# Four score tiles at a time from row tiles, attention reordered by batch, router in column strips

## The reference

```python
q = layernorm(x) @ Wq.T;  k, v = split(ctx @ Wkv_expand.T)
scores = einsum('bhqd,bhkd->bhqk', q, k) / sqrt(32)      # causal, so 100 keys
x = x + tanh(g_xattn) * ((softmax(scores) @ v) @ Wout.T)
h = layernorm(x)
e = argmax(sigmoid(h @ router_w));  p = max(sigmoid(h @ router_w))
x = x + tanh(g_ffn) * p * ((silu(h @ gate_w[e]) * (h @ up_w[e])) @ down_w[e])
```

## Time and profile before

| | us |
|---|---|
| median of 3 runs | 558.25 (558.22 to 561.51) |
| the profiled run, its own time | 560.19 |
| its span, first to last instruction | 558.7 |
| TensorE busy | 508.5 (91%) |
| VectorE, ScalarE, GpSimd busy | 349.5, 303.6, 185.4 |

### The profile page before, as it was taken

How to read it: one execution, slowest core, us unless ns; L and a number is a source line. 1 busy time by engine, 2 the same in 40 slices (tenths; PEclk the granted TensorE clock), 3 DMA queues, 4 the chain that set the end, 5 groups by cost and what they waited for, 6 DMA issues and landing times.

```text
span 558.7 us, 11407 instructions
## 1 busy us (share of the span) xinstructions
PE 508.5 (91%) x3724; PEld 423.9 (76%) x3724; DVE 349.5 (63%) x745; ACT 303.6 (54%) x855; POOL 185.4 (33%) x210
## 2 busy tenths in 40 slices
PE   0999999999999999976489999999999999999991
PEld 0976686768665866656489999999999999999980
DVE  3678568756885556686446666757566665766731
ACT  0799648765786568522134554545454644545520
POOL 5534304631572147233532233224122241220211
PEclk9999999999999999995599999999999999999996
DMA  7500032103310031073428676887677797776610
GB/s 195 169 8 2 16 90 88 61 16 90 89 48 25 15 91 59 18 245 115 104 81 246 212 237 184 262 248 210 199 240 220 212 283 205 205 244 195 224 54 29
DMA packets 58910, 77.30 MB, mean 138 GB/s; under 512 B 5074, under 2 KB 40506, under 8 KB 58880
## 3 DMA queue, kind: packets, MB, share of 16 engines
q1 hardware_dynamic: 53728, 66.90, 40.2%
q0 software_dynamic: 5152, 10.03, 6.3%
HBM read 67.76 MB, written 10.34 MB: 140 GB/s over the span
## 4 chain that ended last, share of the span: by engine, by line
PE 71%; DVE 8%; issue 7%; ACT 6%; POOL 3%; DMA 3%; DVEq 0%; ACTq 0%; SPq 0%; POOLq 0%
PE bank L1148 20%; PE bank L1149 20%; PE bank L1150 19%; ACT pr L668 3%; POOL pn L508 3%; PE bank L1243 2%; PE bank L1233 2%; DMA staging<-in_L_xattn_Wq 2%; PE bank L1282 1%; PE bank L1402 1%; PE bank L1252 1%; ACT staging L612 1%; PE bank L1169 1%; PE bank L1290 1%; DVE pT L970 1%
## 5 line engine op out<-in xcount | busy, mean ns | idle before, releaser
L1148 PE MATMUL bank<-x_hi,gu_hi 128*128 128x224 f32 x512 | 142.6, 279 | 2.9 <-ACT qT L744 1.6
L1149 PE MATMUL bank<-x_lo,gu_hi 128*128 128x224 f32 x512 | 141.9, 277 | 0.0
L1150 PE MATMUL bank<-x_hi,gu_lo 128*128 128x224 f32 x512 | 140.3, 274 | 0.0
L1148 PEld LDWEIGHTS bank<-x_hi,gu_hi 128*128 128x128 f32 x512 | 99.2, 194 | 4.6 <-ACT qT L744 1.7
L1149 PEld LDWEIGHTS bank<-x_lo,gu_hi 128*128 128x128 f32 x512 | 99.2, 194 | 1.0
L1150 PEld LDWEIGHTS bank<-x_hi,gu_lo 128*128 128x128 f32 x512 | 99.3, 194 | 0.0
L668 ACT ACTIVATE pr<-bank,nmx 100x100 f32<-100x100 f32 x256 | 85.6, 374 | 15.5 <-DVE nmx L961 12.1
L781 DVE TENSOR_TENSOR gu_lo<-staging,gu_hi 128x1024 fp32r<-128x1024 f32 x64 | 76.6, 1221 | 16.7 <-ACT gu_hi L612 15.6
L612 ACT ACTIVATE gu_hi<-staging 128x1024 fp32r<-128x1024 f32 x64 | 65.7, 1050 | 31.9 <-DMA staging<-in_L_ffn_up_w 20.7
L508 POOL TENSOR_TENSOR pn<-pr,inv 100x400 f32<-100x400 f32 x64 | 54.6, 853 | 77.7 <-DVE inv L954 72.5
L668 ACT ACTIVATION_READ_ACCUMULATOR pr<-bank,nmx 100x1 f32 x256 | 60.2, 236 | 0.0
(11 more groups left out here) (182 smaller groups left out, 963.7 us busy)
## 6 DMA issues: line engine op xcount, KB each, us to landing
staging<-in_L_ffn_gate_w SPq DMA_DIRECT2D x32, 512.0 KB, 5.4
staging<-in_L_ffn_up_w SPq DMA_DIRECT2D x32, 512.0 KB, 7.2
staging<-in_L_ffn_down_w SPq DMA_DIRECT2D x32, 512.0 KB, 4.0
x_rows<-x SPq DMA_DIRECT2D x8, 800.0 KB
xt<-in_x SPq DMA_DIRECT2D x4, 800.0 KB
xr<-in_x SPq DMA_DIRECT2D x16, 200.0 KB
staging<-in_L_xattn_Wq SPq DMA_DIRECT2D x1, 1024.0 KB, 11.5
x<-in_L_xattn_Wout SPq DMA_DIRECT2D x1, 1024.0 KB, 9.7
```

Source lines behind the costliest of these rows:

```text
L1148: nc.tensor.matmul(dst, a[0], b[0], start=first, stop=False)
L1149: nc.tensor.matmul(dst, a[0], b[1], start=False, stop=False)
L1150: return nc.tensor.matmul(dst, a[1], b[0], start=False, stop=last)
```

## The change

Four things are done. **Scores:** keys are kept as they are (`kT`, one copy of 128 rows in place of four of 32 rows; both `memset`s go), and a head's scores are a product of depth 32 at its own row tile of the array. Tile `n` now holds head `r = n % 4` of each of the four 128-row groups; four banks take the four tiles of a batch, and `scores(c, i)` writes all four with 16 products, after four masks. The bank is gained by giving `out_b` one bank, and tokens always go through `misc_b`. **Order:** all lists of `attend` are rewritten batch by batch. **Router:** 16 products of 100 columns into four strips of 32 rows with a router widened by zeros, and one transpose of 128x128 in place of four small ones. **Stores:** the counter `rows_stored` becomes two, and `residual(c, 0)` waits for the second norm of the former chunk's rows.

```diff
@@ -94,8 +94,6 @@
     DEEP = 3
-    SOONER = 2
-    SPARE_FROM = 14
     KEEP = HP + 2
...
-        keys_b = staging[:, 0:KC * CB * HP * S].rearrange("p (m i j s) -> p m i j s", m=KC, i=CB, j=HP)
+        kT = staging[:, 2 * 3 * 1024 - KC * CT:].rearrange("p (m t) -> p m t", m=KC)
...
-        score_b, turn_b, out_b, misc_b = banks[0:3], banks[3:5], banks[5:7], banks[7]
+        score_b, turn_b, out_b, misc_b = banks[0:4], banks[4:6], banks[6], banks[7]
...
             def keep(c, t):
 
                 act.wait_ge(kq_ready.sem, kq_ready.after(c, t + 1))
-                m, bank = t // 2, score_b[(NT + t) % DEEP]
+                m, bank = t // 2, score_b[t % HP]
                 if t % 2 == 0:
-                    for j in range(HP):
-                        r = slice(j * HD, (j + 1) * HD)
-                        ins = copy(keys_b[r, m, :, j, :], bank[r, 0:CT].rearrange("p (i s) -> p i s", i=CB))
+                    ins = copy(kT[:, m, :], bank[:, 0:CT])
...
+                for n in range(NT):
+                    i, r = n // HP, n % HP
+                    exponentials(c, n)
+                    if n == 0:
+                        keep_values(c, CB - 1)
+                    if n in (1, 2, 4, 6) and not last:
+                        split_token(c + 1, n // 2 if n != 1 else 0)
+                    if n == 8 and not last:
                         split_context(c + 1)
...
+                    if 9 <= n < 9 + CB and not first:
+                        keep_normed(c - 1, n - 9)
+                    if r == 0 and i:
+                        split_output(c, i - 1)
+                    if n == 13 and not first:
                         exp_logits(c - 1)
...
-                dve.wait_ge(rows_stored.sem, rows_stored.after(c, 0))
-                nc.vector.scalar_tensor_tensor(out=x1[0:S, i, 0:H], in0=out_b[i % 2][0:S, :], scalar=tanh_x[0:S, 0:1],
+                dve.wait_ge(x1_stored.sem, x1_stored.after(c, 0))
+                if i == 0:
+                    dve.wait_ge(x2_done.sem, x2_done.after(c, 0))
+                nc.vector.scalar_tensor_tensor(out=x1[0:S, i, 0:H], in0=out_b[0:S, :], scalar=tanh_x[0:S, 0:1],
...
+                for i in range(CB):
+                    n = HP * i
+                    row_max(c, n)
+                    if i:
+                        keep_turned(c, n - 1)
+                    row_max(c, n + 1)
+                    if i == 1 and not first:
+                        rows_norm(c - 1, 12, NORM_STEPS)
+                    row_max(c, n + 2)
+                    inverse(c, n)
+                    row_max(c, n + 3)
+                    if i == 0 and not first:
+                        residual(c - 1, CB - 1)
+                    if i == 1 and not last:
+                        split_token(c + 1, 2)
+                    if i == 2 and not last:
                         split_context(c + 1)
...
+                    if i:
+                        low_output(c, i - 1)
+                    inverse(c, n + 1)
+                    keep_turned(c, n)
+                    if i == 0 and not first:
+                        rows_norm(c - 1, 0, 4)
+                    if i == 0 and not last:
+                        split_token(c + 1, 0)
+                    inverse(c, n + 2)
+                    keep_turned(c, n + 1)
+                    if i == 0 and not first:
+                        rows_norm(c - 1, 4, 8)
+                    if i < 2 and not last:
+                        split_token(c + 1, 1 + 2 * i)
+                    inverse(c, n + 3)
...
+                    keep_turned(c, n + 2)
+                    if i == 0 and not first:
+                        rows_norm(c - 1, 8, 12)
+                    if i and not (i == CB - 1 and last):
+                        residual(c, i - 1)
...
+                keep_turned(c, NT - 1)
+                if not first and not last:
+                    for k in range(CHOOSE_STEPS):
+                        settled(choose, c - 1, whole, k)
...
-            def scores(c, n):
-
-                i, m, b = n // KC, n % KC, n % DEEP
+            def mask_scores(c, n):
+
+                i, r = n // HP, n % HP
                 if n == 0:
                     pe.wait_ge(kq_done.sem, kq_done.after(c, 2 * KC))
-                if n >= DEEP:
-                    pe.wait_ge(exp_done.sem, exp_done.after(c, n - DEEP + 1))
-                nc.tensor.matmul(score_b[b][0:S, 0:HP * S], eye[0:S, 0:S], mask[0:S].unsqueeze(1).to_broadcast([S, HP, S]),
-                                 start=True, stop=False)
-                nc.tensor.matmul(score_b[b][0:S, 0:HP * S], qT[:, m, i * S:(i + 1) * S],
-                                 keys_b[:, m, i].rearrange("p j s -> p (j s)"), start=False, stop=True).then_inc(s_ready.sem, 1)
+                elif i:
+                    pe.wait_ge(exp_done.sem, exp_done.after(c, n - HP + 1))
+                nc.tensor.matmul(score_b[r][0:S, 0:KC * S], eye[0:S, 0:S], mask[0:S].unsqueeze(1).to_broadcast([S, KC, S]),
+                                 start=True, stop=False, skip_group_check=True)
+
+            def scores(c, i):
+
+                t = slice(i * S, (i + 1) * S)
+                for m in range(KC):
+                    for r in range(HP):
+                        p = slice(r * HD, (r + 1) * HD)
+                        ins = nc.tensor.matmul(score_b[r][0:S, m * S:(m + 1) * S], qT[p, m, t], kT[p, m, t], start=False,
+                                               stop=m == KC - 1, tile_position=(r * HD, 0), skip_group_check=True)
+                ins.then_inc(s_ready.sem, 1)
...
-                    ins = nc.tensor.matmul(whole.logits, router[:, k, :], x2T[:, k, :], start=k == 0, stop=k == KC - 1)
+                    for i in range(CB):
+                        ins = nc.tensor.matmul(whole.logits[i * HD:(i + 1) * HD, :], router_wide[:, k, :],
+                                               x2T[:, k, i * S:(i + 1) * S], start=k == 0, stop=k == KC - 1,
+                                               tile_position=(0, i * HD), skip_group_check=True)
...
+                for n in range(HP):
+                    mask_scores(c, n)
+                scores(c, 0)
+
+                if not first:
+                    project(c - 1, CB - 1)
+                values(c, CB - 1)
...
+                if not last:
+                    turn_chunk(c + 1, 0)
+                for i in range(CB):
+                    n = HP * i
+                    if i:
+                        turn_probs(c, n - 1)
+                    if i == 1 and not last:
+                        turn_chunk(c + 1, 2)
+                    if i == 2 and not last:
                         turn_context(c + 1)
...
+                    if i:
+                        weigh(c, i - 1)
...
+                    turn_probs(c, n)
+                    if i < CB - 1:
+                        mask_scores(c, n + 4)
+                    if i == 0 and not last:
+                        turn_chunk(c + 1, 1)
+                    if i == 2 and not first:
+                        turn_normed(c - 1, 0, last)
+                    if i:
+                        project(c, i - 1)
...
+                    turn_probs(c, n + 1)
+                    if i == 1 and not last:
+                        turn_chunk(c + 1, 3)
...
+                if not last:
+                    keys_or_queries(c + 1, 4)
+                if not first:
+                    rank(c - 1, whole)
+                weigh(c, CB - 1)
```

More of the change, by code:

```diff
@@ L1297, in turn_logits @@
                 pe.sem_inc(pe_wait_passed, 1)
[L1298 to L1300 removed]
+                nc.tensor.transpose(whole.turned, ex_t[:], ident[:]).then_inc(ex_ready.sem, 1)
             def rank(c, part):
@@ new lines, in attend @@
+                if not last:
+                    keys_or_queries(c + 1, 3)
+                turn_probs(c, NT - 1)
+                if not last:
+                    keys_or_queries(c + 1, 4)
+                if not first:
+                    rank(c - 1, whole)
+                weigh(c, CB - 1)
+                if not last:
+                    for t in range(5, 2 * KC):
+                        keys_or_queries(c + 1, t)
+                    for i in range(CB - 1):
+                        values(c + 1, i)
+                else:
+                    project(c, CB - 1)
```

274 lines of the change are left out of this document (118 added, 156 removed).

## The result

| | before | after |
|---|---|---|
| median, same chip (runs) | 559.28 us (4) | 611.16 us (4; 607.92 to 612.92) |
| ratio, 95% interval | | 1.0915 [1.0855, 1.0976] |
| profiled run: span | 558.7 | 609.0 |
| TensorE busy | 508.5 | 514.5 (84%) |

A forecast was written before the change was run, and what follows sets the result against it. TensorE's list was taken to bound attention; 35 us come off it, but each batch becomes a round trip. Start +1.2, first chunk 0, middle chunks +10.8, last +9.9 make +22: 558.3 becomes 580 us, range 546 to 602.

The forecast's parts named there:

- the prices of the pieces: TensorE times taken for new work: a batch's scores 0.83 us instead of 2.67, the router 0.83 instead of 2.7.
- the rival of serial row tiles: Row tiles don't run at the same time; scores stay at 2.67 us a batch: +29, 609 us; chance 0.07.
- the sum of waits: Waits and work summed batch by batch through the attention, plus the later start: +22 us.
- start: Before the first mask, three values go ahead, the second behind VectorE's split of `Wout`: +1.2 us.
- middle chunks: Chunks two and three of the attention: 125.3 us against 114.5, +10.8.
- last chunk and what follows: Last chunk, first mask to end of half norm: 55.4 us against 45.5, +9.9; routing of last rows and experts: nothing.
- the second tokens: Batch 1 of a middle chunk: 1.3 us before their copy, one bank going through ScalarE, VectorE and TensorE.
- the rival "the clock falls": Half clock, mostly in the last chunk: +11, 591 us; in middle chunks as well, over 640; chance 0.07.
- 15 us of waits a chunk: Waits counted on TensorE's list per middle chunk; they must stay under 9.7 us for the faster side.
- over 640: Time in us if TensorE also ran at half clock in the middle chunks, 46.7 us of work becoming 93.
- The prediction's own sign of being wrong: Middle chunks under 56 us, scores over 2 us, or the lower clock level before the last chunk's end.

The follow-up runs named there:

- the third filling: Changed kernel with repeated mask products in TensorE's waits, more than the second filling's where its trace still showed half clock: 589.88 us (1.0518).
- The four moves: Changed kernel with fourth tokens' transposes ahead of first projection, router ahead of third, residual behind next row maxima, rank behind last weighing: 609.2 us (1.084).
- the old products: Changed kernel's order, banks and router strips, but block-diagonal keys and scores as four products of depth 128 per batch: 628.7 us (1.1194).
- the kernel before with a gap: Kernel before with GpSimd held some 5.3 us per chunk by two memsets between third and fourth normalisation of the probabilities: 586.92 us (1.0473).

## Why the prediction was right and wrong

- **Right: the sign and its mechanism.** TensorE stops being the bound and every batch is a round trip: ScalarE waits 50.8 us for row maxima, before 12.1.
- **Right: the prices of the pieces.** Scores 0.92 for 0.83, router 0.82 for 0.83; the rival of serial row tiles is out.
- **Nearly right: the sum of waits, at the clock it assumed.** With the clock held up by the third filling it is start +1.0 (+1.2 predicted), first chunk +1.0 (0), middle chunks 129.0 against 114.5, +14.5 (+10.8), last chunk and what follows +12.0 (+9.9): +28.5 us of span for +22. That includes what filling costs, and half clock in the last 11 us of the last chunk, which takes 59.2 us for 55.4. From first exponentials to first exponentials the batches of chunk two take 13.0, 13.6, 11.4 and 27.0 us for 11.0, 13.5, 11.7 and 27.0: only the first, with the wait for the second tokens, was summed too low. (Two slips of the working change nothing: its own sums leave 15.3 to 16.5 us of waits a middle chunk, not 15, and the fourth batch adds up to 26.9.)
- **Wrong: the clock.** The step that failed is the rival "the clock falls", 0.07 and mostly for the last chunk, with the forecast's sum made at whole clock throughout. I had counted 15 us of waits a chunk on TensorE's list and gave the clock no part in the middle chunks, because the kernel before has no such stretch in its attention. At one of them, the second tokens, I wrote 1.3 us for ScalarE; TensorE stood 3.83 there. The clock fell in all four chunks, 102 us of the attention were at half clock, and that cost at least 22 us; 28.5 and 22 make up the 50 us of span. The prediction's own sign of being wrong, the lower level before the last chunk's end, came true. It was not half clock all through either (over 640): it comes back some us after each fall, a third to a half of each chunk is low. A row from behind the attention, where the line shows 5, was the nearest row and pointed there.
- **Wrong: the waits as separate items.** The four moves should have given back up to 14.8 us a middle chunk and gave 2 to 4 us in all. Items of such a sum give its total; they don't say what removing one brings.
- **Not seen: the price of a step of look-ahead,** 31 us with three tiles turned into two. It would have warned from the outset that 9 us of TensorE's work a chunk may not pay for a batch that starts with none ready.

What stays open: how the 67 us of order, banks and strips divide between the round trip, the single output bank and the clock (low is 60 us there, so 30 at most for the clock); and whether four row tiles at once let the clock fall more easily than full products. Behind the same wait of 3.83 us in chunks two and three it stays low 7 us with the old products and 14 and 17 in after. The lost 13 of 29 us may be that, or only the more idle time of a shorter list. In the first three chunks of the filled kernel they ran at whole clock.

## What to carry to other kernels

When a change takes work off the engine that bounds, ask first what the kernel becomes: if TensorE will wait for some us at a time, make the sum a second time with a part of each chunk at half clock (here it was a third to a half), and don't leave that case at a few per cent. Count how many tiles stand ready ahead of the slowest handover before and after; losing one may cost more than the products saved. Take the part of a change that needs no new order (here the router's strips, 0.9896) by itself.

## What the runs showed of the hardware

- Sixteen float32 products of 32 rows by 100 columns in four row tiles occupy TensorE 0.92 us, eight in two row tiles 0.88. Each row tile gets four products in both: the time goes with these, not with the total.
- The granted clock fell to its lower level not only behind a stall (3.83 us in the changed kernel, 4.28 in the kernel before with a gap). It also fell while scores ran in row tiles two at a time and TensorE was no less busy (5.88 of 8 us) than with the full products of depth 128 (5.81), which held it. So in these runs the kind of product counts too; whether by its depth or by the changes of tiling is not separated.
- In the kernel before, four falls cost 10.6 us behind gaps of 16.5; in the changed kernel, filling the waits with products that change nothing won back 22 us.
- The Trainium skill, TensorEngine Tiling (Array Packing), "Gotcha 1: PSUM Pressure", says that row tiles must write to different banks and raise the pressure on them. No run here puts two into one bank; what the trace shows is the price of the banks: look-ahead in pairs, and one output bank in fours.
